# Convolution taps in pairs over 128 rows, and a new order of the front of a fused Mamba block and quantised convolution block

## What is computed

```python
x = x + _L0_conv_ref(_gn(x), ...)      # gated state-space block
x = x + _L1_conv_ref(_gn(x), ...)      # two quantised 3x3 convolutions
```

```python
zxbcdt = u @ in_proj_w.T                       # z0, x0, z, xBC (64+32+32), dt (4 heads)
dt = softplus(dt + dt_bias)
xpad = pad(xBC, 3 tokens ahead)
xconv = silu(conv_b + sum(xpad[:, k:k+L, :] * conv_w[:, k] for k in range(4)))
xs, Bm, Cm = xconv[..., :64], xconv[..., 64:96], xconv[..., 96:]
hstate = hstate * exp(dt*A) + dt * xs * Bm;    y = hstate . Cm      # scan over 256 tokens
```

## Time and profile before

| | |
|---|---|
| median of 3 runs | 68.89 us (68.42 to 71.41) |
| the profiled execution | 68.96 us, of which the span is 67.2 us |
| busy: TensorE, VectorE, ScalarE, GpSimd | 56.7, 50.5, 36.2, 25.5 us |
| mean granted TensorE clock | 0.941 of full speed |
| read from memory | 2.32 MB |

### The profile page before, as it was taken

The page is one execution under the profiler, slowest core; times in us unless marked ns, Lnnn a source line. Parts: engine busy times, 40 slices in busy tenths (PEclk is TensorE's granted clock), DMA queues, the critical chain, the costliest instruction groups (busy, mean ns, idle before and its releaser), DMA issues.

```text
span 67.2 us, 2423 instructions
## 1 busy us (share of the span) xinstructions
PE 56.7 (84%) x1018; PEld 34.7 (52%) x1018; DVE 50.5 (75%) x133; ACT 36.2 (54%) x82; POOL 25.5 (38%) x61
## 2 busy tenths in 40 slices
PE   2996769999999989999999999947558999995900
PEld 0334268545848347549569946614147344494600
DVE  2054694895389998999999687399875879999740
ACT  0454199944695990358876005932995804568000
POOL 5987478780004101036999786000006032000000
PEclk9999999559999999999999999999999658999996
DMA  0899910000000000000000000000000000000045
GB/s 0 274 336 312 396 65 0 10 0 0 0 0 0 5 0 10 0 5 10 0 10 0 0 10 0 10 0 0 0 0 5 10 0 0 0 0 0 10 146 166
DMA packets 2011, 3.00 MB, mean 45 GB/s; under 512 B 208, under 2 KB 1232, under 8 KB 2000
## 3 DMA queue, kind: packets, MB, share of 16 engines
q1 hardware_dynamic: 1424, 1.83, 8.4%
q10 hardware_dynamic: 576, 1.02, 4.2%
HBM read 2.32 MB, written 0.52 MB: 42 GB/s over the span
## 4 chain that ended last, share of the span: by engine, by line
PE 64%; DVE 13%; ACT 9%; DMA 5%; issue 3%; DVEq 1%; SPq 1%; ACTq 0%
PE ps L298 9%; PE ps L338 8%; PE ps L506 5%; DMA vc<-vec_in 5%; PE ps L427 5%; PE ps L620 4%; PE ps L374 3%; PE ps L321 3%; PE ps L547 3%; PE ps L515 3%; PE ps L531 3%; PE ps L411 2%; PE ps L399 2%; ACT L710 2%; DVE ell L913 2%
## 5 line engine op out<-in xcount | busy, mean ns | idle before, releaser
L298 PE MATMUL ps<-zbf 128*128 128x512 bf16 x35 | 11.4, 486 | 1.3 <-DVE zbf L847 1.3
L913 DVE TENSOR_TENSOR_SCAN ell<-ps,delta 128x512 f32<-128x512 f32 x8 | 9.2, 1208 | 0.8 <-PE ps L399 0.7
L298 PEld LDWEIGHTS ps<-zbf 128*128 128x128 bf16 x35 | 4.0, 123 | 6.6 <-issue 3.3
L338 PE MATMUL ps<-u,wtap 64*32 64x256 f32 x128 | 5.4, 469 | 0.3 <-ACT bc L710 0.3
L620 PE MATMUL ps<-h,wk 64*64 64x256 bf16 x144 | 4.7, 275 | 0.9 <-DVE h L1115 0.8
L1214 POOL TENSOR_SCALAR sc<-sc 128x1 f32<-128x1 f32 x1 | 4.9, 4926 | 0.1
L620 PEld LDWEIGHTS ps<-h,wk 64*64 64x64 bf16 x144 | 3.8, 106 | 1.9 <-issue 1.5
L961 DVE TENSOR_TENSOR mm<-ell,gsb 128x1024 f32<-128x1024 f32 x4 | 4.6, 1208 | 0.0
L346 PE MATMUL ps<-u,wtap 64*64 64x512 f32 x32 | 4.5, 613 | 0.0
L506 PEld LDWEIGHTS ps<-mm,xdz 64*32 64x32 f32 x256 | 3.3, 106 | 1.3 <-issue 1.2
L745 ACT ACTIVATE ysq<-yg 128x512 f32<-128x512 f32 x2 | 1.3, 631 | 4.9 <-DVE yg L980 4.9
(11 more groups left out here) (252 smaller groups left out, 141.4 us busy)
## 6 DMA issues: line engine op xcount, KB each, us to landing
w1n<-c1n_in ACTq DMA_DIRECT2D x1, 288.0 KB, 3.9
w2t<-c2t_in SPq DMA_DIRECT2D x1, 288.0 KB, 6.4
w1t<-c1t_in SPq DMA_DIRECT2D x1, 288.0 KB, 6.7
x_sb<-x_in ACTq DMA_DIRECT2D x1, 256.0 KB, 3.4
x_sb<-x_in SPq DMA_DIRECT2D x1, 256.0 KB, 3.2
cw_sb<-cw_in SPq DMA_DIRECT2D x1, 256.0 KB, 5.9
out<-o_sb SPq DMA_DIRECT2D x1, 256.0 KB, 2.6
out<-o_sb SPq DMA_DIRECT2D x2, 128.0 KB, 1.9
```

What stands on the lines that cost most here:

```text
L298: mul(ps[:, bank, :], zbf[:, 0:P], zbf[:, :], start=True, stop=True)
L338: last = mul(ps[q:q + 32, BC[j], bank_col:bank_col + TOK], wtap[half(h), k, at:at + 32], u[half(h), 2 * j + b, k:k + TOK], start=(k == 0), ...
L913: vec_.tensor_tensor_scan(dst, ps[:, SPREAD[g % 2], :], delta[:, :], 0.0, ALU.mult, ALU.add).then_inc(scanned, 1)
```

## The change

- A second copy of x comes from memory as `xt_in` (128 x 2 halves x 4 images x 256 tokens, made on the host): its rows 0 to 63 hold x one token late, its rows 64 to 127 hold x, and it has this for both halves of the batch. It is loaded as two transfers of 512 KB, one on SyncE's queue ahead of `w2t` and `w1t`, one on ScalarE's ahead of `w1n` and `wb`; `cst` grows by 64 KB and goes ahead of `w1n`; `cw` shrinks from 256 to 128 KB.
- `rstd` and `nbias` are brought to all 128 rows for each half by two products with a 64 x 128 matrix (`rw_wide`), copied by VectorE to `rw`. From it `ut` = xt * rstd + nbias is made in eight pieces of 128 x 256: two by VectorE, six by GpSimd, ahead of GpSimd's masks. VectorE then waits for all of them and sets one column to zero (`ut_ready`).
- The taps go in pairs: one product over 128 rows does taps 2m and 2m + 1, m = 0 and 1. The x projection has 8 products instead of 16, in tiles of 128 rows x 64 columns; B and C have 16 instead of 32 each, in tiles of 128 x 32.
- The whole of x and then B are projected ahead of the step sums; C is in one piece ahead of spread 6. The decay rows (L384) come ahead of all four prefix sums of j = 0. One more `keep_warm` product is issued. On ScalarE the silu of C moves ahead of the copy `bt`; on TensorE the second part of `x_to_tokens` moves behind spread 7.

The diff, cut to what matters:

```diff
+            sp.dma_start(xt_sb[:, 0, :, :], xt[:, 0, :, :]).then_inc(ld_xt0, 16)
             sp.dma_start(w2t[:, :], c2t).then_inc(ld_w2t, 16)
...
-            keep_warm(5)
-
+            keep_warm(6)
+            pe.wait_ge(ld_cst, 16)
+            pe.wait_ge(nbias_ready, 1)
+            for h in range(2):
+                s = slice(CH * h, CH * h + CH)
+                last = mul(ps[:, RWB[h], 0:8], cs[s, K_DUP:K_DUP + P], rn[s, :, :].rearrange("p e b -> p (e b)"),
+                           start=True, stop=True, tile_position=(CH * h, 0))
+            last.then_inc(rw_wide, 1)
...
+            for h, j, p in halves:
+                if 2 * h + j:
+                    pe.wait_ge(ut_pool, 4 * h + 2 * j)
+                for m in range(2):
+                    last = mul(ps[half(p), XS[j], :], wtap[:, m, A_XS:A_XS + CH], ut[:, h, 2 * j:2 * j + 2, 2 * m:2 * m + TOK],
+                               start=(m == 0), stop=(m == 1), tile_position=(0, CH * p))
+            last.then_inc(xs_proj, 1)
+            state_projection(A_B).then_inc(b_proj, 1)
...
-            pe.wait_ge(dt_wide, 1)
-            prefix(0, 0, 1)
...
-            prefix(0, 2, 3).then_inc(prefix_sums, 1)
+            pe.wait_ge(dt_wide, 1)
+            prefix(0, 0, 1, 2, 3).then_inc(prefix_sums, 1)
...
-            x_projection(1)
...
-            state_projection(A_C, TOK, range(0, 2))
+            state_projection(A_C).then_inc(c_proj, 1)
...
+            dve.wait_ge(rw_wide, 1)
+            vec_.tensor_copy(rw[:, :, :, :].rearrange("p h e b -> p h (e b)"), ps[:, RWB[0]:RWB[1] + 1, 0:8]).then_inc(rw_ready, 1)
...
+            dve.wait_ge(ut_dve, 2)
+            dve.wait_ge(ut_pool, 6)
+            vec_.memset(ut[0:CH, :, :, 2:3], 0.0).then_inc(ut_ready, 1)
...
+            for h, b in ((0, 2), (0, 3), (1, 0), (1, 1), (1, 2), (1, 3)):
+                gp.tensor_scalar(ut[:, h, b, 2:TP], xt_sb[:, h, b, :], rw[:, h, 0, b:b + 1], rw[:, h, 1, b:b + 1],
+                                 ALU.mult, ALU.add).then_inc(ut_pool, 1)
+            pool.wait_ge(ut_pool, 6)
```

More of the change, by code:

```diff
@@ L80, with build @@
 UP = TAPS - 1 + TOK
-def build(nc, x, wa, cw, wb, vec, cst, c1n, c1t, c2t, out):
+TP = TAPS - 2 + TOK
+def build(nc, x, xt, wa, cw, wb, vec, cst, c1n, c1t, c2t, out):
     with ExitStack() as ctx:
@@ L103, in build @@
         one_row = cs[0:1, K_HALF:K_HALF + CH]
-        cw_sb = sb("cw_sb", [P, TAPS * A_TAP])
-        wtap = sb("wtap", [P, TAPS, A_TAP])
+        cw_sb = sb("cw_sb", [P, 2 * A_TAP])
+        wtap = sb("wtap", [P, 2, A_TAP])
+        xt_sb = sb("xt_sb", [P, 2, HALF_B, TOK])
+        ut = sb("ut", [P, 2, HALF_B, TP])
+        rw = sb("rw", [P, 2, 2, HALF_B])
+        rn = sb("rn", [P, 2, HALF_B])
+        rstd, nbias = rn[:, 0, :], rn[:, 1, :]
         u = sb("u", [P, HALF_B, UP])
@@ L215, in build @@
             sem(n) for n in ("ld_x0", "ld_x1", "ld_wa", "ld_cw", "ld_vec", "ld_cst", "ld_wb"))
+        ld_xt0, ld_xt1, rw_wide, rw_ready, ut_dve, ut_pool, ut_ready = (
+            sem(n) for n in ("ld_xt0", "ld_xt1", "rw_wide", "rw_ready", "ut_dve", "ut_pool", "ut_ready"))
         ld_w1n, ld_w1t, ld_w2t = (sem(n) for n in ("ld_w1n", "ld_w1t", "ld_w2t"))
@@ L328, in half, with state_projection @@
                 return slice(CH * p, CH * p + CH)
[L330 to L334, removed]
+            def state_projection(at):
+                for m in range(2):
                     for h, j, p in halves:
@@ L337, in state_projection @@
                             q = 32 * (2 * p + b)
-                            last = mul(ps[q:q + 32, BC[j], bank_col:bank_col + TOK], wtap[half(h), k, at:at + 32],
-                                       u[half(h), 2 * j + b, k:k + TOK], start=(k == 0), stop=(k == TAPS - 1),
-                                       tile_position=(CH * h, q))
-                return last
[L343 to L350, removed]
+                            last = mul(ps[q:q + 32, BC[j], TOK * (at == A_C):TOK * (at == A_C) + TOK], wtap[:, m, at:at + 32],
+                                       ut[:, h, 2 * j + b, 2 * m:2 * m + TOK], start=(m == 0), stop=(m == 1), tile_position=(0, q))
+                return last
+            pe.wait_ge(tap_ready, 1)
+            pe.wait_ge(ut_ready, 1)
+            pe.wait_ge(ut_dve, 2)
+            for h, j, p in halves:
+                if 2 * h + j:
+                    pe.wait_ge(ut_pool, 4 * h + 2 * j)
+                for m in range(2):
+                    last = mul(ps[half(p), XS[j], :], wtap[:, m, A_XS:A_XS + CH], ut[:, h, 2 * j:2 * j + 2, 2 * m:2 * m + TOK],
+                               start=(m == 0), stop=(m == 1), tile_position=(0, CH * p))
+            last.then_inc(xs_proj, 1)
+            state_projection(A_B).then_inc(b_proj, 1)
             pe.wait_ge(var_ready, 1)
@@ L653, in _ @@
             act.wait_ge(nbias_ready, 1)
-            act.wait_ge(zero_u, 1)
             for b in (1, 3):
@@ L1253, in constants, with tap_pairs @@
     return c
+def tap_pairs(x):
+    x = x.reshape(2, HALF_B, CH, TOK).transpose(2, 0, 1, 3)
+    o = np.zeros((2, CH, 2, HALF_B, TOK), np.float32)
+    o[0, :, :, :, 1:] = x[:, :, :, :-1]
+    o[1] = x
+    return o.reshape(P, 2, HALF_B, TOK)
 def twice(w):
@@ L1309 @@
         "x_in": np.asarray(x).reshape(2, HALF_B, CH, TOK).transpose(0, 2, 1, 3).reshape(P, HALF_B, TOK),
-        "wa_in": wa, "cw_in": np.tile(cw.T.reshape(1, TAPS * A_TAP), (P, 1)), "wb_in": wb, "vec_in": vec, "cst_in": constants(),
+        "xt_in": tap_pairs(np.asarray(x)), "wa_in": wa,
+        "cw_in": np.repeat(cw.T.reshape(2, 2, A_TAP).transpose(1, 0, 2), CH, axis=0).reshape(P, 2 * A_TAP), "wb_in": wb, "vec_in": vec, "cst_in": constants(),
         "c1n_in": np.tile(w1.reshape(CH, W33), (2, 1)),
```

38 lines of the change are left out of this document (21 added, 17 removed).

## The result

The changed kernel takes 76.97 us (median of 4 runs, 76.21 to 77.40) where the kernel before takes 68.87 (68.42 to 71.41): a ratio of 1.116, with a 95% interval of 1.102 to 1.131. The forecast was 75.2. Some executions of each kernel take 1.5% or more longer than its fastest; every ratio here is of means without them, while the medians are of all runs. The profiled execution took 77.29 us with a span of 75.6, so 8.3 us more than that of before.

What follows compares the result with a forecast made beforehand. TensorE's queue was taken to bound the kernel up to the first scan, VectorE behind it. The profiled 68.96 us + 5.8 (first scan at 24.5 instead of 18.73) + 0.4 behind it gave 75.2 us; range 71.3 to 78.8.

Steps and rivals of the forecast that it cites:

- What bounds the front, and what the change puts there: Ahead of the first scan: TensorE's queue sets the front; x and B there take 5.4 us plus 1.95 for half clock.
- The start of the pieces: GpSimd's start on ut: rw at about 9.4 us, copy landed near 9.5, start at 9.5, half a microsecond later possible.
- The pieces: GpSimd's six operations making ut: 0.60 us each, 3.6 in all (2.4 to 7.2), plus 0.35 beside VectorE.
- The gap and the clock: TensorE idle 2.6 us before x, then half clock for 3.9 us of dense work, costing 1.95 us (0 to 2.5).
- What is late next: Behind B: softplus parts (19.6 us) and GpSimd's delta (19.9) ready in time; 3.58 us on to the first scan, 24.5.
- Behind the first scan: Taps leaving TensorE worth at most 0.42 us, scan 6 later by 0.9; +0.4 us in sum (-0.4 to +0.9).
- The rival *faster: Behind the first scan, the three taps' 3.0 us come off TensorE in full: 67.4 us; chance 4%.
- The range: Time of the whole changed kernel: 71.3 to 78.8 us, meant to leave out no more than 2 in 10.
- long pieces: Rival on GpSimd's making of ut: 1.2 us a piece, first scan at 28.1, 78.8 us in all; chance 15%.

Runs made afterwards that it cites:

- e6: The kernel before, with all four taps of x (old products) and then B ahead of the step sums: 72.38 us, ratio 1.058.
- e8: The kernel before with 9 instead of 5 products of zeros ahead of the dt projection: 68.16 us, ratio 0.994 (0.977 to 1.010).
- e1: The changed kernel without the two transfers of the delayed copy, ut made from x itself: 74.28 us, ratio 1.079.
- e3: The changed kernel with 16 products of zeros in TensorE's gap ahead of the x projection: 77.18 us (75.85 to 78.15).
- e5: e1 with GpSimd's six pieces cut from 256 to 2 columns each, the rest of ut zero: 74.45 us, ratio 1.088.
- e2: The changed kernel with the copy's two transfers issued early, cw, wb and the 3x3 weights behind them: 76.12 us, ratio 1.096.
- e10: The changed kernel with C in its old two parts and ScalarE's order as before: 79.33 us, ratio 1.155.
- e12: The changed kernel's pairs with B behind spread 1, x behind spreads 3 and 4, ut made later, copy loaded last, gap filled: 75.83 us, no clear ratio.
- e9: e5 with 11 products of zeros between spreads 1 to 5: 76.39 us (74.25 to 77.21).
- e7: The kernel before with the copy's two transfers added and nothing reading them: 71.18 us against 70.17.

## Why the prediction was right

**What bounds the front, and what the change puts there: right.** x and B stand ahead of the step sums and are paid in full: x and B together took 7.36 us (16.80 to 24.16) and were forecast at 5.4 + 1.95 = 7.35. e6 shows the order by itself at about 4 us of time. That TensorE was the bound by only 0.8 us, and the softplus chain the next, e8 bears out.

**The start of the pieces: the mis-sized term.** The prediction put the landing "near 9.5", "level with `rw`", and with it GpSimd's start. It started at 12.87, 3.4 us later. Two things were off. `rw` came at 10.76 rather than 9.4, since the warm products ran at 457 ns each and ended at 10.1; e1, where nothing but `rw` is waited for, starts its pieces 0.2 us behind it. So about 1.5 us of the 3.4 would have been there with the copy landed in time. The other 1.9 are the SyncE half of the copy, landed at 12.5. The estimate took one rate, 0.31 MB/us, and the order of issue, as if the transfers ended in that order: 2.15 MB by 9.5 us. They did not: the ScalarE half landed at about 10, but that of SyncE, with 9.9 us from issue to landing, hardly ahead of `w2t` and `w1t`, which were issued behind it and took 10.3 and 10.6. "Half a microsecond later is possible" was far too little. x then began 3.2 us later than forecast, and the first scan 2.8.

**The pieces: right, and both terms of it.** 3.6 + 0.35 us were forecast for six, 3.62 measured. The first two stood beside VectorE's pieces and its product `wtap` and took 0.78 and 0.70 us; the other four took 0.55 each:

```profile
13.65 0.70 POOL L1177 TENSOR_SCALAR ut<-xt_sb,rw 128x256 f32<-128x256 f32 x1
14.34 0.55 POOL L1177 TENSOR_SCALAR ut<-xt_sb,rw 128x256 f32<-128x256 f32 x1
```

That is 0.38 us for standing beside VectorE. In e3 only the first piece was held up, and took 1.11. VectorE pays as well: `wtap` took 0.62 us here, and 0.42 in e3 and e5. The fixed part is most of a piece: in e5 the last four, two columns wide, took 0.34 each. From the rate of the Trainium skill ("GPSIMD Engine Reference", § 3.1) 256 columns are an estimated 0.22 us without the dispatch, which leaves that part out; about 0.2 us is also what the columns added here (0.55 - 0.34).

**The gap and the clock: right in kind, the size by luck.** 4.37 us idle: the forecast 2.6, 3.2 for the late start, less 1.4 because `dt` ended later, at 12.42. The clock was at half when x began and back at 20.49, 3.7 us later; 3.9 were taken over from the kernel before. That figure is no constant: the same products had run at half clock for 2.8 us in e5, 4.2 in e2 and 5.5 in e1 when it came back. e3 confirms the gap as the cause, and the size at the place, 1.7 us for x; it also shows that filling the gap gave no measurable time.

**What is late next: right.** The parts were ready at 21.98, 2.2 us before B ended; `delta` at 22.87 was hidden. From the end of B to the first scan 3.16 us, forecast 3.58. First scan: 24.5 forecast, 27.32 measured: 3.2 from the late start of x, less 0.4 of this tail.

**Behind the first scan: right in kind.** The taps that left TensorE bought nothing, as VectorE was full: at full clock it is 47.9 us from the first scan to the end with them there (e8) and without (e6). Scan 6 waits 1.02 us for C in one piece, where it waited 0.19: 0.83, forecast 0.9. The stretch changed by -0.2, forecast +0.4 within -0.4 to +0.9. Even the +0.4 is there once stretches with a full clock are compared, +0.3 to +0.5 (see e10); half a microsecond of it is hidden in these two executions by the low clock that only the one before had. The rival *faster*, which needed -2.8, is out. That the median is only 1.8 us over the forecast with the scan 2.8 later is two smaller terms of the other sign: this 0.6 between +0.4 and -0.2, and the profiled run, 0.3 above its median.

**The range.** 76.97 lies within 71.3 to 78.8, but the upper end had been set for long pieces of 1.2 us, which did not come. That a start 3.4 us too late still fell inside is luck.

**What stays open.** Of the 8.1 us, about 4 are the order (e6) and 2.7 the transfers (e1). The rest, between 1 and 2, is left for the making of `ut` by subtraction; no experiment shows it. e5 should have and didn't: its time is e1's (74.45 against 74.28), and part of what its front gained was lost behind the scan with the clock. In e1, e5, e10 and e12 the part behind the scan was 1.0 to 5.2 us longer than in the changed kernel, with the clock at half in places (in e12 with more work, too), and which kernel meets that could not be foretold. In e3 and e9 it was 0.95 and 0.6 us longer at full clock, each with a pause of TensorE that has no cause in the profile.

## What to carry to other kernels

Two half-height products that ran side by side in two row tiles take the same time as one over all rows (four taps of about 1 us each, and 3.7 to 3.9 us for the eight products in pairs): stacking taps over 128 rows saves instructions, not streaming, and its price is a second copy to load and prepare. Ask of work moved ahead of the first use of the engine that bounds the kernel what it holds up there, since relief for an engine beside the bound is worth only the bound's idle time (0.42 us of 19.4 here). And a transfer that the front waits for is issued ahead of all that it doesn't need (in e2 the pieces started 1.9 us earlier so, though the time shows no clear gain); a landing time is read per queue, from the rows of what shares it, not from one mean rate.

## What the hardware showed that I had not expected

- **When the clock first comes up differs from execution to execution.** Ahead of `dt` the zero products took 250 ns each in the kernel before, and 457 in the changed one, in e1 and in e3, though the clock row of the page is at 9 there. The trace's first record of the granted clock begins at 4.7 us in the kernel before and at 10.3 in the changed one, and the page counts what lies ahead of it as full. In e10, which is the changed kernel up to that point, it begins at 5.5; in e7 only at 17.2. `dt` began at 10.5 instead of 9.0. Not every difference in the first 10 us is the kernel's.
- **Half clock behind the first scan comes without a visible reason.** In e5 the clock fell after 28.40, TensorE ran C and spread 6 at 0.50, and scan 6 waited 2.26 us for it. TensorE had had 3.73 us of work in the 6.31 before; the changed kernel has 3.74 in the same stretch, and its clock stayed full.
- **Two transfers of the same size on two queues** took 8.3 and 9.9 us; the later one was issued 0.9 us later, with more behind it. With `cw` and the weights all behind them (e2), they landed after 8.1 and 8.5.
- **A GpSimd operation with two scalars from memory** took 0.55 us for 256 columns and 0.34 for 2 with nothing of VectorE's in its way, some 0.8 ns a column on top of a fixed 0.34. Beside VectorE either engine can be the one that loses: the changed kernel's first two pieces took 0.78 and 0.70, while in e12, beside the softplus chain, all six took 0.55 and three of VectorE's steps of 64 columns took 0.45 to 0.50 instead of 0.23:

```profile
10.91 3.23 POOL L1198 TENSOR_SCALAR ut<-xt_sb,rw 128x256 f32<-128x256 f32 x6 [1.83 <-DMA xt_sb<-xt_in]
```
